# Products by high and low parts: passes on the high part first, and the wait for the low part at its own pass

## The chip, the cores and the metric

The kernel runs on one core of one Trainium2 chip. The metric is the device time of one execution in microseconds (us); three executions of the kernel before gave 998.48, 1000.50 and 1000.87 us, with a median of 1000.5 us. Lower is better.

## What is computed

One decoder layer over x (16 batch rows of 256 tokens, 256 features, float32), with a context of the same shape. Three blocks follow one another, each with a residual:

```python
x = x + causal_linear_attention(layernorm(x)) @ w_proj.T      # block a: 16 heads, chunks of 128
x = x + xattn(layernorm(x), ctx, ctx)                         # block b: cross attention on tanh
                                                              # "probabilities", then an MLP 256-1024-256
x = x + ffn(layernorm(x))                                     # block c: the 128 best-scored tokens of 256 go
                                                              # through attention and a gated MLP 256-682-256
# inside block c
_, idx = top_k(x @ w_router, 128);  x_sel = x[idx]
x_proc = x_sel + x_attn + (silu(h2 @ W1.T) * (h2 @ W2.T)) @ W3.T
out = x.at[idx].set(x_proc)
```

Which tokens are selected depends on small differences of scores, so several products are computed more exactly than one reduced-precision pass would allow.

## The kernel before

**High and low parts.** An operand of such a product is held as two tiles: a high part, the value rounded to the format that TensorE (PE) reads in one go (`..._hi`), and a low part, what the rounding left over (`..._lo`). A product takes three passes: high x high, high x low, low x high (`PASSES`, L1037). Weights are split once at the start. Activations are split each time: ScalarE (ACT) copies the value into the high tile, and then VectorE (DVE) subtracts that from the value to give the low tile. For the input of the attention's output projection the subtraction is done by GpSimd (POOL, `a_ylo_`). So a low part is always ready later than its high part.

**Stages and steps.** All weights stay on chip. One iteration works on one batch row in each block, with blocks a, b and c working on different rows. Each block is cut into named steps (`a_q`, `b_down_0`, `c_scat` and so on). The string `ORDER` lists all steps of an iteration; a "+" behind a name means that the step belongs to a row that started one iteration earlier. Each engine issues its own steps in that order, with waits on semaphores for what other engines deliver. Nothing else sets the order: there is no scheduler. There are three iterations or so of filling up, a hardware loop, and an emptying phase in which block a, then block b have nothing left to do.

**The steps that matter here, on PE.**

- `a_q` (L1072): queries of block a; waits for high part `a_thi`, low part `a_tlo`, then 12 matmuls into bank 1 in two halves. `a_k` and `a_val` follow with the same inputs.
- `a_proj` (L1156): projection of block a; waits for `a_yhi` (ACT) and `a_ylo` (POOL), then 12 matmuls.
- `b_up_j` and `b_down_j` (j = 0 to 3): the MLP of block b, 12 matmuls each. `b_down_j` waits for `b_ghi` and `b_glo`.
- `c_gu_0`: the first piece of the gated MLP, 12 matmuls of 384 columns into banks 6 and 7; waits for `c_h2hi`, `c_h2lo`.
- `c_ff_0`, `c_ff_1`: the last product of the gated MLP, 9 matmuls each; waits for `c_gthi`, `c_gtlo`.
- `c_scat` (L1417): puts the selected rows back at their places by a product with a 0/1 matrix, which has only a high part. There are two output halves of 128 tokens, with a high and a low pass each: 4 matmuls. It waits for `c_yhi` and `c_ylo`.

**Around `c_scat`.** PE runs `c_ff_1`, `a_q`, `c_scat`, `a_k`, in this order. When `c_ff_1` is done, DVE adds the residual (`c_y`, L1002), ACT copies the high part (`c_yhi`), and DVE computes `b_vq` (L835, block b) and then the low part `c_ylo` (L714). DVE goes on with `c_normed` (L729), which needs nothing of PE, then with `c_done` (L1011), which waits for `c_scat`, and with `c_rscore` (L917, the router's scores). In turn PE waits for `c_rscore` before `c_sbc`, and the chain to the next selection goes on from there.

Of the kernel before, what the change touches and what calls it, by code (L numbers as in the profile page):

```python
# [14 lines left out]
B, T, D = 16, 256, 256  # L15
P = 128
TT = T // P
DC = D // P
# [3 lines left out]
FF = 682  # L22
# [82 lines left out]
def decoder(nc, x, ctx_in, ctx_t, consts, vec_bc, vec_cols, w_a, w_proj, w_diff, w_1, w_2, w_cqk, w_cv, w_out, w_gu, w_3, out):  # L105
    ctx = ExitStack()
    with ctx:
# [37 lines left out]
        a_tr = pair("a_tr", [P, DC, T])  # L145
# [24 lines left out]
        b_s0 = pair("b_s0", [P, 512])  # L170
# [31 lines left out]
        c_hs = pair("c_hs", [P, DC, R])  # L202
# [26 lines left out]
        a0, a1, a2, b0, b1, c0, c1, c2 = bank  # L229
# [49 lines left out]
        b_up, b_gelu, b_ghi, b_glo, b_down = sig("b_up", 4), sig("b_gelu", 8), sig("b_ghi", 4), sig("b_glo", 4), sig("b_down", 4)  # L279
# [43 lines left out]
        GATE = ((c1, c2, 0, 3 * P), (c0, c1, 3 * P, FF - 3 * P))  # L323
# [711 lines left out]
        def _(pe):  # L1035
            mm = nc.tensor.matmul
            PASSES = ((0, 0), (0, 1), (1, 0))  # L1037

            def split_product(out_, lhs, rhs, n):

                for a, (p, q) in enumerate(PASSES):
                    for k in range(n):
                        last = mm(out_, lhs(p, k), rhs(q, k), start=a == 0 and k == 0, stop=a == 2 and k == n - 1)  # L1043
                return last
# [21 lines left out]
            def by_features(which, bk):  # L1066
                for m in range(DC):
                    last = split_product(bk[:, m * T:(m + 1) * T],
                                         lambda p, k: wa[p][:, k, which * D + m * P:which * D + (m + 1) * P],
                                         lambda p, k: a_tr[p][:, k, :], DC)  # L1070
                return last

            def a_q_(b):
                weights(b, LOADS_A)
                pe.wait_ge(*a_thi(b))
                pe.wait_ge(*a_tlo(b))
                if not first(b):
                    pe.wait_ge(*a_done(b - 1))
                by_features(0, a1).then_inc(a_qk.sem, 1)

            def a_k_(b):
                by_features(1, a2).then_inc(a_qk.sem, 1)
# [72 lines left out]

            def a_proj_(b):  # L1156
                pe.wait_ge(*a_yhi(b))
                pe.wait_ge(*a_ylo(b))
                for t in range(TT):
                    last = split_product(a1[:, t * D:(t + 1) * D], lambda p, k: a_tr[p][:, k, t * P:(t + 1) * P],  # L1160
                                         lambda p, k: wp[p][:, k, :], DC)
                last.then_inc(a_proj.sem, 1)


            upcoming = iter(range(len(loads)))
# [59 lines left out]
            def mlp_up(j):  # L1225
                def step(b):
                    if j == 0:
                        weights(b, LOADS_A + LOADS_B)
                        pe.wait_ge(*b_hhi(b))
                        pe.wait_ge(*b_hlo(b))  # L1230
                    else:
                        pe.wait_ge(*b_gelu(b, 2 * j))
                    for n in range(2):
                        f = 2 * j + n
                        last = split_product(b0[:, n * T:(n + 1) * T], lambda p, k: w1[p][:, k, f * P:(f + 1) * P],
                                             lambda p, k: b_s0[p][:, k * T:(k + 1) * T], DC)
                    last.then_inc(b_up.sem, 1)
                return step

            def mlp_down(j):  # L1240
                def step(b):
                    part = (b_s2, b_s1)[j % 2]
                    if j == 0:
                        pe.wait_ge(*b_fput(b))
                        if not final(b):
                            pe.wait_ge(*a_scput(b + 1))
                    pe.wait_ge(*b_ghi(b, j + 1))
                    pe.wait_ge(*b_glo(b, j + 1))
                    for t in range(TT):
                        for a, (p, q) in enumerate(PASSES):  # L1250
                            for n in range(2):
                                last = mm(b1[:, t * D:(t + 1) * D], part[p][:, n * T + t * P:n * T + (t + 1) * P],  # L1252
                                          w2[q][:, 2 * j + n, :], start=j == 0 and t == 0 and a == 0 and n == 0,
                                          stop=j == 3 and a == 2 and n == 1, skip_group_check=True)
                    last.then_inc(b_down.sem, 1)
                return step

# [110 lines left out]
            def c_h2tp_(b):  # L1368
# [2 lines left out]
                    last = nc.tensor.transpose(c0[:, c * R:(c + 1) * R], c_h2[:, c * P:(c + 1) * P], ident)  # L1371
                last.then_inc(c_h2tp.sem, 1)

            def gate_product(bk, which, j):
                at, n = GATE[j][2:]
                return split_product(bk[:, 0:n], lambda p, k: c_hs[p][:, k, :],
                                     lambda p, k: wgu[p][:, k, which * FF + at:which * FF + at + n], DC)

            def c_gu_0_(b):
                weights(b, len(loads))  # L1380
                pe.wait_ge(*c_h2hi(b))
                pe.wait_ge(*c_h2lo(b))
                pe.wait_ge(*c_h2put(b))
                gate_product(c1, 0, 0)
                gate_product(c2, 1, 0).then_inc(c_gu.sem, 1)

            def c_gu_1_(b):
                gate_product(c0, 0, 1).then_inc(c_gu.sem, 1)
# [14 lines left out]
            def c_ff_(j):  # L1403
                def step(b):
                    pe.wait_ge(*c_gthi(b, j + 1))
                    pe.wait_ge(*c_gtlo(b, j + 1))
                    if j == 0:
                        pe.wait_ge(*c_gate(b))
                    for a, (p, q) in enumerate(PASSES):
                        for k in range(3 * j, 3 * j + 3):  # L1410
                            last = mm(c1[:, 0:D], act_t[p][:, k, :], w3[q][:, k, :], start=j == 0 and a == 0 and k == 0,
                                      stop=j == 1 and a == 2 and k == 5, skip_group_check=True)
                    if j:
                        last.then_inc(c_ff.sem, 1)
                return step

            def c_scat_(b):  # L1417
                pe.wait_ge(*c_yhi(b))
                pe.wait_ge(*c_ylo(b))
                for t in range(TT):  # L1420
# [78 lines left out]
```

## Time and profile before

| | |
|---|---|
| median of three executions | 1000.5 us |
| the profiled execution | 998.39 us |
| its span, first to last instruction | 996.6 us |
| outside the span | 1.8 us |
| PE busy with matmuls | 862.5 us (87%), 7488 matmuls |
| PE weight loads (overlap the matmuls) | 749.4 us (75%), 7488 loads |
| DVE busy | 718.2 us (72%) |
| ACT busy | 596.5 us (60%) |
| POOL busy | 222.6 us (22%) |
| mean granted clock of PE over the span | 0.969 |
| chain of work that ended last | PE 55%, DVE 27%, issue 9%, ACT 6% |

The chain of work is found by walking back from the last instruction, at each step to what released it. A share of 55% for PE and 27% for DVE says that the end is set by the two in turns: PE in some stretches, DVE in others. In such a chain "issue" is time in which the engine waited for nothing that the profile shows, the way of a semaphore among it. Matmul rows overlap: a row's duration is longer than the distance to the next one's start, and the distance says how fast PE works. The weight loads have rows of their own (PEld).

### The profile page before, as it was taken

The numbers are of one execution on the slowest core, as the hardware profiler recorded it, in microseconds if no ns is written. First come the engines' busy times: TensorE is split into PE (matmuls) and PEld (weight loads), VectorE is DVE, ScalarE is ACT, GpSimd is POOL, SyncE is SP. The second block draws the span as 40 slices with busy tenths as digits, with TensorE's granted clock in tenths as the row PEclk, the third lists the DMA queues.
The fourth block names the chain that finished last, engine by engine and source line by source line (L and its number), as shares of the span: only waits on it lengthen the run. The fifth ranks groups of instructions, "written<-read, shape, count | busy, mean of one in ns | idle before, by whom it ended". The sixth has DMA issues, their size and how long they took to land.

```text
span 996.6 us, 21602 instructions
## 1 busy us (share of the span) xinstructions
PE 862.5 (87%) x7488; PEld 749.4 (75%) x7488; DVE 718.2 (72%) x1670; ACT 596.5 (60%) x1581; POOL 222.6 (22%) x379
## 2 busy tenths in 40 slices
PE   3668898989989998989989998989989998977856
PEld 2547788787969788787969788787969788766745
DVE  4677778787777778787777778787777778664432
ACT  3165666757475766757475766757475766635432
POOL 0121422131312222131312222131312222131100
PEclk9788999999999999999999999999999999998968
DMA  6131000101010100100010100001010100000000
GB/s 227 44 88 32 23 12 12 33 12 32 0 42 0 32 11 11 32 11 32 0 42 0 32 11 11 32 11 32 0 42 0 32 11 21 12 2 11 1 12 11
DMA packets 20320, 25.03 MB, mean 25 GB/s; under 512 B 1472, under 2 KB 17856, under 8 KB 20288
## 3 DMA queue, kind: packets, MB, share of 16 engines
q1 hardware_dynamic: 18848, 20.33, 6.4%
q10 hardware_dynamic: 1440, 4.28, 1.4%
q8 instruction: 19, 0.31, 0.1%
q14 instruction: 13, 0.11, 0.0%
HBM read 20.41 MB, written 4.19 MB: 25 GB/s over the span
## 4 chain that ended last, share of the span: by engine, by line
PE 55%; DVE 27%; issue 9%; ACT 6%; POOL 1%; DMA 1%; DVEq 0%; ACTq 0%; SPq 0%; POOLq 0%
PE bank L1043 15%; PE bank L1252 8%; PE bank L1131 4%; DVE a_s L788 3%; PE bank L1297 3%; PE bank L1217 3%; PE bank L1209 3%; PE bank L1149 2%; PE bank L1285 2%; PE bank L1322 2%; DVE before L929 2%; ACT L602 2%; PE bank L1336 2%; PE bank L1051 2%; PE bank L1111 2%
## 5 line engine op out<-in xcount | busy, mean ns | idle before, releaser
L639 ACT ACTIVATE w_raw_or_stage_c<-bank,c_nmax 128x128 f32<-128x128 f32 x256 | 90.9, 375 | 27.7 <-DVE c_nmax L960 27.7
L960 DVE TENSOR_REDUCE c_nmax<-bank 128x4 f32<-128x512 f32 x64 | 42.2, 682 | 74.9 <-PE bank L1322 74.9
L602 ACT ACTIVATE prob<-bank,b_folded 128x256 f32<-128x256 f32 x128 | 53.7, 471 | 48.6 <-PE bank L1043 46.3
L788 DVE TENSOR_TENSOR a_s<-bank,const 128x512 f32<-128x512 f32 x112 | 71.7, 677 | 13.1 <-PE bank L1131 11.2
L413 POOL TENSOR_TENSOR a_tr_lo<-a_norm,a_tr_hi 128x512 fp32r<-128x512 f32 x16 | 20.7, 1292 | 260.8 <-ACT a_tr_hi L490 260.8
L714 DVE TENSOR_TENSOR b_s_lo<-prob,b_s_hi 128x512 fp32r<-128x512 f32 x64 | 44.1, 690 | 33.6 <-ACT b_s_hi L490 33.6
L1043 PE MATMUL bank<-b_s_hi,w_mlp_hi 128*128 128x256 f32 x256 | 56.8, 304 | 6.4 <-ACT prob L602 5.8
L678 ACT ACTIVATE w_raw_or_stage_c<-bank,c_rms_half 128x384 f32<-128x384 f32 (+1 forms) x32 | 17.5, 547 | 69.6 <-PE bank L1043 46.8
L389 POOL TENSOR_TENSOR x<-x,vectors_by_row 128x512 f32<-128x512 f32 x16 | 21.5, 1344 | 155.1 <-DVE w_raw_or_stage_c L954 155.1
L490 ACT ACTIVATE b_s_hi<-prob 128x512 fp32r<-128x512 f32 x64 | 40.5, 633 | 24.8 <-PE bank L1252 21.0
L639 ACT ACTIVATION_READ_ACCUMULATOR w_raw_or_stage_c<-bank,c_nmax 128x1 f32 x256 | 54.6, 213 | 0.0
L1131 PE MATMUL bank<-qT_by_parity,kT 32*128 32x256 f32 x512 | 38.6, 416 | 17.3 <-DVE a_e L788 9.8
L778 DVE RECIPROCAL a_e<-a_e 128x512 f32<-128x512 f32 x16 | 53.5, 3342 | 0.0
L1252 PE MATMUL bank<-w_mlp_hi,b_s_hi 128*128 128x256 f32 x256 | 52.1, 284 | 0.0
L1252 PE MATMUL bank<-w_mlp_hi,b_s_lo 128*128 128x256 f32 x256 | 50.6, 279 | 0.0
L1043 PE MATMUL bank<-b_s_lo,w_mlp_hi 128*128 128x256 f32 x256 | 50.6, 279 | 0.0
L1252 PE MATMUL bank<-w_mlp_lo,b_s_hi 128*128 128x256 f32 x256 | 50.5, 278 | 0.0
L1043 PE MATMUL bank<-b_s_hi,w_mlp_lo 128*128 128x256 f32 x256 | 50.4, 278 | 0.0
L1043 PEld LDWEIGHTS bank<-b_s_hi,w_mlp_hi 128*128 128x128 f32 x256 | 40.1, 190 | 12.5 <-ACT prob L602 9.7
L1336 PE MATMUL bank<-const,w_raw_or_stage_c 128*128 128x128 f32 x256 | 41.7, 287 | 6.3 <-ACT w_raw_or_stage_c L639 5.4
L490 ACT ACTIVATE w_raw_or_stage_c<-bank 128x512 f32<-128x512 f32 x32 | 19.8, 620 | 43.7 <-PE bank L1336 43.7
L1131 PEld LDWEIGHTS bank<-qT_by_parity,kT 32*128 32x128 f32 x512 | 24.9, 192 | 25.0 <-DVE a_e L788 13.7
(242 smaller groups left out, 2843.1 us busy)
## 6 DMA issues: line engine op xcount, KB each, us to landing
x_in<-in_x SPq DMA_DIRECT2D x16, 256.0 KB, 2.8
qc<-in_ctx SPq DMA_DIRECT2D x16, 256.0 KB, 2.9
b_f<-in_ctx_t SPq DMA_DIRECT2D x16, 256.0 KB, 2.7
out<-w_raw_or_stage_c SPq DMA_DIRECT2D x16, 256.0 KB, 2.2
w_raw_or_stage_c<-in_w ACTq DMA_DIRECT2D x4, 512.0 KB, 5.1
w_raw_or_stage_c<-in_w_gu ACTq DMA_DIRECT2D x4, 341.0 KB, 3.0
w_raw_or_stage_c<-in_w_a SPq DMA_DIRECT2D x2, 384.0 KB, 5.9
w_raw_or_stage_c<-in_w ACTq DMA_DIRECT2D x2, 384.0 KB, 3.3
```

The lines of the kernel that those rows point to most:

```text
L490: act_in(out_, in_, ACT.Copy, scale=scale).then_inc(done.sem, 1)
L602: act_in(prob[:, 2 * (j % 2) + n, :], b0[:, n * T:(n + 1) * T], ACT.Gelu, bias=b1p[:, f:f + 1]).then_inc(b_gelu.sem, 1)
L639: act_in(c_e[g % 2][:, j * R:(j + 1) * R], (c1, c2)[g % 2][:, j * R:(j + 1) * R], ACT.Exp, bias=c_nmax[:, n:n + 1], accum_out=c_den[:, hea ...
L714: tt(out_, full, high.bitcast(F32), ALU.subtract).then_inc(done.sem, 1)
L778: nc.vector.reciprocal(a_e1[:, :], a_e1[:, :]).then_inc(a_dinv.sem, 1)
L788: tt(heads(A_MASKED[t][n][:, :]), heads(A_SCORES[n][:, :]), tri.unsqueeze(1).broadcast_to([P, 4, P]), ALU.mult).then_inc(a_scput.sem, 1)
L960: nc.vector.tensor_reduce(c_nmax[:, 4 * g:4 * g + 4], heads((c1, c2)[g % 2][:, :]), axis=AX.X, op=ALU.max, negate=True).then_inc(c_max.sem, 1)
L1043: last = mm(out_, lhs(p, k), rhs(q, k), start=a == 0 and k == 0, stop=a == 2 and k == n - 1)
L1131: last = mm(A_SCORES[n][:, 2 * c * P:2 * (c + 1) * P], kT[r:r + 32, c, t * P:(t + 1) * P], qM[r:r + 32, c, t, :, :].rearrange("p m q -> p ...
L1209: last = mm(b0[:, m * T:(m + 1) * T], prob[:, k, m * P:(m + 1) * P], prob[:, TT + k, :], start=k == 0, stop=k == DC - 1)
L1252: last = mm(b1[:, t * D:(t + 1) * D], part[p][:, n * T + t * P:n * T + (t + 1) * P], w2[q][:, 2 * j + n, :], start=j == 0 and t == 0 and a ...
L1336: last = nc.tensor.transpose(c0[:, j * R:(j + 1) * R], c_e[g % 2][:, j * R:(j + 1) * R], ident)
```

## The change

A new helper, `some_passes`, runs a given list of passes over all output halves, pass by pass, instead of all three passes of one half and then those of the next. Passes are split into those that read only the high part of the activation and those that read its low part. The wait for the low part moves from the head of the step to the place between the two groups. Matmuls, weight loads, semaphores and the order of the steps are the same in number; only PE's instructions change.

```diff
+            HIGH_LEFT, LOW_LEFT = ((0, 0), (0, 1)), ((1, 0),)
+            HIGH_RIGHT, LOW_RIGHT = ((0, 0), (1, 0)), ((0, 1),)
+
+            def some_passes(passes, outs, lhs, rhs, n, begin=False, end=False):
+
+                for a, (p, q) in enumerate(passes):
+                    for o, out_ in enumerate(outs):
+                        for k in range(n):
+                            last = mm(out_, lhs(o, p, k), rhs(o, q, k), start=begin and a == 0 and o == 0 and k == 0,
+                                      stop=end and a == len(passes) - 1 and k == n - 1, skip_group_check=True)
+                return last
...
             def a_q_(b):
                 weights(b, LOADS_A)
                 pe.wait_ge(*a_thi(b))
+                if not first(b):
+                    pe.wait_ge(*a_done(b - 1))
...
+                some_passes(HIGH_RIGHT, *args, begin=True)
                 pe.wait_ge(*a_tlo(b))
-                if not first(b):
-                    pe.wait_ge(*a_done(b - 1))
-                by_features(0, a1).then_inc(a_qk.sem, 1)
+                some_passes(LOW_RIGHT, *args, end=True).then_inc(a_qk.sem, 1)
...
             def a_proj_(b):
                 pe.wait_ge(*a_yhi(b))
...
+                some_passes(HIGH_LEFT, *args, begin=True)
                 pe.wait_ge(*a_ylo(b))
-                for t in range(TT):
-                    last = split_product(a1[:, t * D:(t + 1) * D], lambda p, k: a_tr[p][:, k, t * P:(t + 1) * P],
-                                         lambda p, k: wp[p][:, k, :], DC)
-                last.then_inc(a_proj.sem, 1)
+                some_passes(LOW_LEFT, *args, end=True).then_inc(a_proj.sem, 1)
...
                     pe.wait_ge(*b_ghi(b, j + 1))
+                    some_passes(HIGH_LEFT, *args, begin=j == 0)
                     pe.wait_ge(*b_glo(b, j + 1))
...
+                    last = some_passes(LOW_LEFT, *args, end=j == 3)
...
             def c_scat_(b):
                 pe.wait_ge(*c_yhi(b))
-                pe.wait_ge(*c_ylo(b))
-                for t in range(TT):
-                    for part in range(2):
+                for part in range(2):
+                    if part == 1:
+                        pe.wait_ge(*c_ylo(b))
+                    for t in range(TT):
                         last = mm(c2[:, t * D:(t + 1) * D], sel_t[:, t * P:(t + 1) * P], flat(c_hs[part][:, :, :]),
-                                  start=part == 0, stop=part == 1)
+                                  start=part == 0 and t == 0, stop=part == 1, skip_group_check=True)
                 last.then_inc(c_scat.sem, 1)
```

`c_gu_0` is rewritten in the same manner (high passes on banks 6 and 7 by turns, wait for `c_h2lo`, low passes on both), and in `c_ff_j` the wait for `c_gtlo` moves ahead of the third pass, with no matmul moved. `b_up_j` changes only the order of its passes; both its waits stay at its head.

First place, on PE: `c_scat` (bank 7) between `a_q` (bank 1) and `a_k` (bank 2). Before:

```order
L1043 MATMUL bank1<-a_tr_hi,w_attn_lo 128x256 x2
L1422 MATMUL bank7<-c_hs_hi,select_by_rank 128x256 [waits c_ylo,c_yhi]
L1422 MATMUL bank7<-c_hs_lo,select_by_rank 128x256
L1422 MATMUL bank7<-c_hs_hi,select_by_rank 128x256
L1422 MATMUL bank7<-c_hs_lo,select_by_rank 128x256
L1043 MATMUL bank2<-a_tr_hi,w_attn_hi 128x256 x2
```

And now on PE, at the same place in the program:

```order
L1047 MATMUL bank1<-a_tr_lo,w_attn_hi 128x256 [waits a_tlo]
L1047 MATMUL bank1<-a_tr_lo,w_attn_hi 128x256 x3
L1448 MATMUL bank7<-c_hs_hi,select_by_rank 128x256 [waits c_yhi]
L1448 MATMUL bank7<-c_hs_hi,select_by_rank 128x256
L1448 MATMUL bank7<-c_hs_lo,select_by_rank 128x256 [waits c_ylo]
L1448 MATMUL bank7<-c_hs_lo,select_by_rank 128x256
L1055 MATMUL bank2<-a_tr_hi,w_attn_hi 128x256 x2
```

Both matmuls on the high part stand ahead of the wait for `c_ylo`, and both on the low part behind it.

Second place, on PE: `a_proj` in the filling phase (bank 1; the tile `a_tr` holds the attention's output here). Before:

```order
L1043 MATMUL bank1<-w_proj_hi,a_tr_hi 128x256 [waits a_ylo,a_yhi]
L1043 MATMUL bank1<-w_proj_hi,a_tr_hi 128x256
L1043 MATMUL bank1<-w_proj_lo,a_tr_hi 128x256 x2
L1043 MATMUL bank1<-w_proj_hi,a_tr_lo 128x256 x2
L1043 MATMUL bank1<-w_proj_hi,a_tr_hi 128x256 x2
```

And now, the whole step on PE:

```order
L1047 MATMUL bank1<-w_proj_hi,a_tr_hi 128x256 [waits a_yhi]
L1047 MATMUL bank1<-w_proj_hi,a_tr_hi 128x256 x3
L1047 MATMUL bank1<-w_proj_lo,a_tr_hi 128x256 x4
L1047 MATMUL bank1<-w_proj_hi,a_tr_lo 128x256 [waits a_ylo]
L1047 MATMUL bank1<-w_proj_hi,a_tr_lo 128x256 x3
```

Eight matmuls stand ahead of the wait for `a_ylo` and four behind it; before, all twelve stood behind it.

## Rows read from the trace of the kernel before

**Rows 1.** One iteration: us, then busy us and count by engine, PE clock.

```profile
499.25:555.32 56.07, 51.85 (x467) 45.52 (x467) 43.59 (x104) 36.56 (x99) 13.57 (x23) 1.00 0.06 19
```

**Rows 2.** PE's waits over the whole span: us in total, times, longest us.

```profile
PE bank L1422 <- DVE c_hs_lo L714: 18.5, 16, 2.4
...
PE bank L1043 <- POOL a_tr_lo L413: 3.9, 2, 3.1
...
PE bank L1043 <- DVE a_tr_lo L714: 1.5, 1, 1.5
...
PE bank L1043 <- DVE c_hs_lo L714: 1.0, 1, 1.0
...
PE bank L1411 <- DVE gated_t_lo L714: 0.8, 1, 0.8
```

**Rows 3.** Chain of work at `c_scat`, iteration of rows 1: start us, us, what.

```profile
554.79 0.39 DVE c_hs_lo L714
555.18 0.14 issue
555.32 0.72 PE bank L1422 x4
```

**Rows 4.** Timeline there: start us, us, engine, line, operation [idle before, releaser].

```profile
554.28 0.42 ACT L490 ACTIVATE c_hs_hi<-c_h 128x256 fp32r<-128x256 f32 x1 [2.85 <-DVE c_h L1002]
...
555.08 0.73 DVE L729 TENSOR_SCALAR w_raw_or_stage_c<-x,c_mv,c_rs 128x256 f32<-128x256 f32 x2
...
555.32 0.35 PE L1422 MATMUL bank<-c_hs_hi,select_by_rank 128*128 128x256 f32 x1 [1.01 <-DVE c_hs_lo L714]
...
555.51 0.28 PE L1422 MATMUL bank<-c_hs_lo,select_by_rank 128*128 128x256 f32 x1
...
555.63 0.28 PE L1422 MATMUL bank<-c_hs_hi,select_by_rank 128*128 128x256 f32 x1
...
555.86 0.41 PE L1043 MATMUL bank<-a_tr_hi,w_attn_hi 128*128 128x256 f32 x2
...
556.06 0.69 DVE L1011 TENSOR_TENSOR w_raw_or_stage_c<-w_raw_or_stage_c,bank 128x512 f32<-128x512 f32 x1 [0.25 <-PE bank L1422]
```

**Rows 5.** Timeline of PE: last pass of `b_up_3`, then `b_down_1` with both waits.

```profile
538.44 0.39 PE L1043 MATMUL bank<-b_s_hi,w_mlp_lo 128*128 128x256 f32 x2
538.67 0.39 PE L1252 MATMUL bank<-w_mlp_hi,b_s_hi 128*128 128x256 f32 x2
538.90 0.39 PE L1252 MATMUL bank<-w_mlp_lo,b_s_hi 128*128 128x256 f32 x2
```

**Rows 6.** Chain of work in the filling phase: first `a_q`, first and second `a_proj`.

```profile
14.36 0.61 ACT a_tr_hi L490
...
15.83 4.86 PE bank L1043 x24
...
41.56 0.64 ACT a_tr_hi L490
...
43.68 2.91 PE bank L1043 x12
...
88.83 0.65 ACT a_tr_hi L490
```

**Rows 7.** Timeline of PE at the second `a_proj`.

```profile
90.97 0.47 PE L1043 MATMUL bank<-w_proj_hi,a_tr_hi 128*128 128x256 f32 x2 [0.77 <-POOL a_tr_lo L413]
```

**Rows 8.** Timeline of the emptying phase: `c_ff_1`, `c_y`, `c_gu_0`, `c_ff_0`.

```profile
943.72 0.59 PE L1411 MATMUL bank<-w_ffn_hi,gated_t_hi 128*128 128x256 f32 x3 [0.79 <-DVE gated_t_lo L714]
...
945.06 0.42 DVE L1002 TENSOR_TENSOR c_h<-bank,c_h 128x256 f32<-128x256 f32 x1 [0.49 <-PE bank L1411]
...
981.04 0.38 ACT L490 ACTIVATE c_hs_hi<-bank 128x256 fp32r<-128x256 f32 x1 [0.16 <-PE bank L1371]
...
981.99 0.59 PE L1043 MATMUL bank<-w_ffn_gu_hi,c_hs_hi 128*128 128x384 f32 x2 [0.98 <-DVE c_hs_lo L714]
...
988.28 0.59 PE L1411 MATMUL bank<-w_ffn_hi,gated_t_hi 128*128 128x256 f32 x3 [0.31 <-issue]
```

More of the change, by code:

```diff
@@ L1075, in a_q_ @@
                 pe.wait_ge(*a_thi(b))
-                pe.wait_ge(*a_tlo(b))
                 if not first(b):
                     pe.wait_ge(*a_done(b - 1))
-                by_features(0, a1).then_inc(a_qk.sem, 1)
+                args = ([a1[:, m * T:(m + 1) * T] for m in range(DC)], lambda m, p, k: wa[p][:, k, m * P:(m + 1) * P],
+                        lambda m, p, k: a_tr[p][:, k, :], DC)
+                some_passes(HIGH_RIGHT, *args, begin=True)
+                pe.wait_ge(*a_tlo(b))
+                some_passes(LOW_RIGHT, *args, end=True).then_inc(a_qk.sem, 1)
             def a_k_(b):
@@ L1157, in a_proj_ @@
                 pe.wait_ge(*a_yhi(b))
+                args = ([a1[:, t * D:(t + 1) * D] for t in range(TT)],
+                        lambda t, p, k: a_tr[p][:, k, t * P:(t + 1) * P], lambda t, p, k: wp[p][:, k, :], DC)
+                some_passes(HIGH_LEFT, *args, begin=True)
                 pe.wait_ge(*a_ylo(b))
-                for t in range(TT):
-                    last = split_product(a1[:, t * D:(t + 1) * D], lambda p, k: a_tr[p][:, k, t * P:(t + 1) * P],
-                                         lambda p, k: wp[p][:, k, :], DC)
-                last.then_inc(a_proj.sem, 1)
+                some_passes(LOW_LEFT, *args, end=True).then_inc(a_proj.sem, 1)
             upcoming = iter(range(len(loads)))
@@ L1232, in step @@
                         pe.wait_ge(*b_gelu(b, 2 * j))
[L1233 to L1237, printed above, removed]
+                    args = ([b0[:, n * T:(n + 1) * T] for n in range(2)],
+                            lambda n, p, k: w1[p][:, k, (2 * j + n) * P:(2 * j + n + 1) * P],
+                            lambda n, p, k: b_s0[p][:, k * T:(k + 1) * T], DC)
+                    some_passes(HIGH_RIGHT + LOW_RIGHT, *args, begin=True, end=True).then_inc(b_up.sem, 1)
                 return step
@@ L1246, in step @@
                             pe.wait_ge(*a_scput(b + 1))
+                    args = ([b1[:, t * D:(t + 1) * D] for t in range(TT)],
+                            lambda t, p, n: part[p][:, n * T + t * P:n * T + (t + 1) * P],
+                            lambda t, p, n: w2[p][:, 2 * j + n, :], 2)
                     pe.wait_ge(*b_ghi(b, j + 1))
+                    some_passes(HIGH_LEFT, *args, begin=j == 0)
                     pe.wait_ge(*b_glo(b, j + 1))
-                    for t in range(TT):
[L1250 to L1254, printed above, removed]
+                    last = some_passes(LOW_LEFT, *args, end=j == 3)
                     last.then_inc(b_down.sem, 1)
@@ L1372, in c_h2tp_ @@
                 last.then_inc(c_h2tp.sem, 1)
+            GATE_ARGS = [(bk[:, 0:GATE[0][3]], lambda p, k: c_hs[p][:, k, :],
+                          lambda p, k, w=w: wgu[p][:, k, w * FF + GATE[0][2]:w * FF + GATE[0][2] + GATE[0][3]])
+                         for w, bk in enumerate((c1, c2))]
             def gate_product(bk, which, j):
@@ L1381, in c_gu_0_ @@
                 pe.wait_ge(*c_h2hi(b))
-                pe.wait_ge(*c_h2lo(b))
-                pe.wait_ge(*c_h2put(b))
-                gate_product(c1, 0, 0)
-                gate_product(c2, 1, 0).then_inc(c_gu.sem, 1)
+                pe.wait_ge(*c_h2put(b))
+                for a, (p, q) in enumerate(HIGH_LEFT):
+                    for bk, lhs, rhs in GATE_ARGS:
+                        for k in range(DC):
+                            mm(bk, lhs(p, k), rhs(q, k), start=a == 0 and k == 0, stop=False, skip_group_check=True)
+                pe.wait_ge(*c_h2lo(b))
+                for p, q in LOW_LEFT:
+                    for bk, lhs, rhs in GATE_ARGS:
+                        for k in range(DC):
+                            last = mm(bk, lhs(p, k), rhs(q, k), start=False, stop=k == DC - 1, skip_group_check=True)
+                last.then_inc(c_gu.sem, 1)
             def c_gu_1_(b):
@@ L1405, in step @@
                     pe.wait_ge(*c_gthi(b, j + 1))
-                    pe.wait_ge(*c_gtlo(b, j + 1))
                     if j == 0:
                         pe.wait_ge(*c_gate(b))
-                    for a, (p, q) in enumerate(PASSES):
+                    for a, (p, q) in enumerate(HIGH_LEFT + LOW_LEFT):
+                        if a == 2:
+                            pe.wait_ge(*c_gtlo(b, j + 1))
                         for k in range(3 * j, 3 * j + 3):
```

1 line of the change is left out of this document (removed).

## The prediction, made before the changed kernel ran

> **What bounds the kernel now.** I read the table of an iteration first. Iterations repeat every 56.07 us and PE has a matmul under way for 51.85 of it, at a granted clock of 1.00 [rows 1]. So PE has some 4 us of gaps per iteration, and whatever closes one counts only if the rest of the loop can follow. Second, I read PE's waits, because the change does nothing but let PE begin before a low part is there. The list is the key to the sum: only one wait for a low part recurs, `c_scat` for `c_hs_lo`, 16 times and 18.5 us in all. The other waits for low parts came once or twice in the whole run: 3.9 us for GpSimd's part at `a_proj`, 1.5 us at `a_q`, 1.0 us at `c_gu_0`, 0.8 us at `c_ff` [rows 2]. In the steady iterations `a_q`, `a_proj`, all `b_down` and `c_gu_0` find their low part ready, so the moved waits there have nothing to give back. Third, the chain of work: it passes through `c_scat`, coming from DVE's low part and going back to DVE [rows 3], so a shorter `c_scat` is worth something there, but only as far as DVE can use it.
>
> **`c_scat`, in each of 16 rows.** The wait of about 1 us does not go away; its end stays where DVE's low part puts it. The high part's copy starts at 554.28 and takes 0.42, so it is there at 554.70 [rows 4]. The way from a finished part to the first matmul is 0.14 [rows 3], so PE could begin the high passes at 554.84. A first matmul after a wait is followed by the next one 0.19 later (555.32 to 555.51), and the further ones at 0.12 (555.51 to 555.63) [rows 4]: both high passes have been issued by 554.84 + 0.19 + 0.12 = 555.15, ahead of 555.32. At 555.32 only two low passes are left. Before, four took from 555.32 to 555.86, where `a_k` begins: 0.54. Two take 0.19 + 0.12 = 0.31. The gain is 0.23 per row, not 1.0.
>
> Can the others use 0.23? DVE stood idle for 0.25 before `c_done`, waiting for `c_scat`; its own `c_normed`, begun at 555.08 and 0.73 long, ends at 555.81, so `c_done` can start at 555.83 instead of 556.06 [rows 4]. It just fits: 0.25 is the most that this place can yield, 0 the least (if something else than `c_scat` holds DVE there). I take 0.23. What follows on DVE (scores, comparison, selection) comes in an unbroken chain, and PE's `a_k` moves by the same 0.23, so nothing overtakes. 16 rows x 0.23 = 3.7 us; bounds 0 and 4.0.
>
> **The filling phase.** These are single places, on the chain of work [rows 6].
> - First `a_q`: the high part ended at 14.36 + 0.61 = 14.97; with 0.14 on top PE can begin at 15.11 instead of 15.83. Eight matmuls don't need the low part, more than fit in the time gained, so no second wait comes. Gain 0.72.
> - First `a_proj`: the high part ended at 42.20, start 42.34 instead of 43.68: gain 1.34. Twelve matmuls took 2.91, so the eight high ones are some 1.9, longer than 1.34, and again GpSimd's low part is there when it is needed.
> - Second `a_proj`: the high part ended at 89.48, while PE was still busy; PE's own idle time before it was 0.77 [rows 7]. Eight matmuls at 0.12 are 0.96, so all of 0.77 is filled. Gain 0.77.
> Together 2.8 us. Lower bound 0, if the weight splitting that shares ACT and DVE in this phase takes over; upper bound 2.8, since that is all the time that there is.
>
> **The emptying phase.** [rows 8] `c_ff_1` waited 0.79 and has six high matmuls, about 0.7; but the DVE addition behind it waited only 0.49, so 0.49 counts. `c_gu_0`: high part at 981.04 + 0.38 = 981.42, start 981.56 instead of 981.99: 0.43. The last `c_ff_0` had 0.31 idle before it, and its high part came before: 0.3. Together 1.2 us, bounds 0 and 1.2. The three `c_scat` here are already among the 16.
>
> **What the moved waits cost where they are met.** Each row of the batch passes ten waits inside a product: one in `a_q`, one in `a_proj`, four in `b_down`, one in `c_gu_0`, two in `c_ff`, one in `c_scat`. The trace of before shows no such wait inside these products, but the nearest thing: between the last pair of `b_up_3` and the first of `b_down_1` stand two waits that are already met, and the distance is 0.23 per pair, as it is one pair later without a wait [rows 5]. So a met wait costs 0. At the other end, if it let the pipe run empty, a matmul would be followed only after its own 0.28 instead of 0.12: 0.16 each [rows 4]. Six of the ten (four `b_down`, `a_proj`, `c_gu_0`) stand in stretches where PE sets the pace: 6 x 16 x 0.16 = 15.4 us. I take 0, because the near row is the same case but for the place of the wait.
>
> The Trainium skill, TensorE: Matmul & The Clock Gate, section Back-to-back issue gap, says that the distance of matmuls is set by weight load and matmul together, pipelined through a reorder window; a wait between them could keep the next load from being pulled ahead. The trace agrees for a wait that is not yet met (0.19 against 0.12 after it) and doesn't for met ones [rows 4, 5].
>
> **The order of the passes.** Output halves now change after every second matmul instead of every sixth, in about 130 matmuls per row; in `c_gu_0` the banks alternate. `c_scat` of before changes its half between 555.51 and 555.63 and the distance is the same 0.12 as inside other products; I take 0. Distances in products of unchanged kind vary from 0.115 to 0.12 [rows 4, 5]; if the new order shifted all by these 5 ns, it would be 130 x 16 x 0.005 = 10 us to either side, which I hold to be unlikely.
>
> **Sum.** 3.7 + 2.8 + 1.2 = 7.7 us. Against the profiled execution, 998.39 (span 996.6 and 1.8 around it), that gives 990.7. The profiled one lies 2.1 under the median shown, 1000.5, from which the same gain gives 992.8. I say 992.
>
> **Rivals.**
> 1. The gain at `c_scat` comes, the single places don't: filling is then paced by the splitting of weights, emptying by other chains. For it: DVE has weight work between all these steps. Against: the chain of work runs through exactly these waits. Gain about 4 us: 996.
> 2. Nothing moves: DVE does not start `c_done` earlier, since 0.25 of slack is thin and any delay of `c_normed` eats it; the iteration stays at 56.07. Some part of the filling gain is left, less than 3 us: 998.5. Against it: DVE waited for `c_scat` in 15 of 16 rows by the same pattern.
> 3. Slower: the waits inside `b_down`, `a_proj` and `c_gu_0`, though met, break the pipe. At 0.08 each (6 x 16 x 0.08 = 7.7) they eat all the gain, and above that the kernel is slower; at 0.16 it is 7.7 slower than before, 1008. Against: rows 5. The skill's rule named above points this way; by it, with 0.07 for each (the 0.19 less the 0.12), the sum would be 6.7 of cost against 7.7 of gain, about no change.
> 4. The change of output half makes matmuls a little slower or faster (up to 10 us either way).
>
> **Chances and range.** Forecast as worked out (989 to 995): 0.58. Rival 1: 0.15. Rival 2: 0.09. Rival 3: 0.10. Rival 4: 0.08, split evenly. A measurement of this kernel can tell about 0.3% from no change, 3 us: faster then means below 997.5. Faster: 0.58 + most of rival 1 (0.11) + 0.04 = 0.73. Same: the rest of rival 1, rival 2 and a third of rival 3, 0.16. Slower: 0.11. The range that should hold 8 in 10 takes in rival 1 and most of rival 2, and below the bounds of the gains: 989 to 998.5.
>
> **What would show it.** Iterations of 55.84 instead of 56.07. At `c_scat` two matmuls on `c_hs_hi` about 0.48 ahead of those on `c_hs_lo`, `a_k` some 0.3 after the latter's start, and DVE's idle time before `c_done` down from 0.25 to nearly 0. The first `a_proj` beginning 0.14 after ACT's copy instead of after GpSimd. Pairs of `b_down` 0.23 to 0.24 apart across the wait; anything above 0.28 at that place would speak for rival 3. An iteration of 56.07 or more, with `c_scat` early all the same, would make the forecast wrong.

## The result and the profile after

The changed kernel took 990.06 us (median of 6 runs) against 999.09 us for the kernel before (6 runs): a ratio of 0.9913, 95% interval 0.9888 to 0.9937. The whole interval lies below 1. The forecast was 992.0 us, from a gain of 7.7 us; the medians differ by 9.0 us, and the profiled span went from 996.6 to 987.4 us, a gain of 9.2.

The iteration first, in the same columns as [rows 1]:

```profile
494.11:549.91 55.80, 52.21 (x467) 45.67 (x467) 43.53 (x105) 36.52 (x99) 13.55 (x24) 1.00 0.06 19
```

PE has as many matmuls as before, in 55.80 us instead of 56.07, at the same granted clock. (Its busy time rose by 0.36 because the rows of the two early matmuls of `c_scat` now cover a part of the wait; in e1 below, which changes `c_scat` alone, it is 52.15.) Its waits over the whole span, which answer to [rows 2]:

```profile
PE bank L1448 <- ACT c_hs_hi L490: 9.7, 16, 1.8
...
PE bank L1047 <- ACT a_tr_hi L490: 2.4, 2, 1.6
...
PE bank L1403 <- ACT c_hs_hi L490: 0.5, 1, 0.5
...
PE bank L1436 <- DVE gated_t_lo L714: 0.2, 1, 0.2
```

`c_scat` (now L1448) waits 9.7 us for the high part instead of 18.5 for the low one. Those 8.8 us of waiting are not the gain: the two low passes still can't run before `c_ylo`. In the kernel before, `c_ylo` of [rows 4] stands in the timeline at

```profile
554.75 0.42 DVE L714 TENSOR_TENSOR c_hs_lo<-c_h,c_hs_hi 128x256 fp32r<-128x256 f32 x1
```

The timeline of the changed kernel at the same `c_scat`, against [rows 4]:

```profile
549.43 0.42 ACT L490 ACTIVATE c_hs_hi<-c_h 128x256 fp32r<-128x256 f32 x1 [2.84 <-DVE c_h L1002]
...
549.90 0.50 PE L1448 MATMUL bank<-c_hs_hi,select_by_rank 128*128 128x256 f32 x2 [0.44 <-ACT c_hs_hi L490]
549.91 0.42 DVE L714 TENSOR_TENSOR c_hs_lo<-c_h,c_hs_hi 128x256 fp32r<-128x256 f32 x1
550.24 0.73 DVE L729 TENSOR_SCALAR w_raw_or_stage_c<-x,c_mv,c_rs 128x256 f32<-128x256 f32 x2
...
550.38 0.50 PE L1448 MATMUL bank<-c_hs_lo,select_by_rank 128*128 128x256 f32 x2
...
550.72 0.40 PE L1055 MATMUL bank<-a_tr_hi,w_attn_hi 128*128 128x256 f32 x2
...
550.92 0.69 DVE L1011 TENSOR_TENSOR w_raw_or_stage_c<-w_raw_or_stage_c,bank 128x512 f32<-128x512 f32 x1
```

Two things became shorter. From the first low matmul to `a_k` it is 0.34 (forecast 0.31), where four matmuls took 0.54: 0.20 less. And the first low matmul starts 0.47 after the start of `c_ylo` (549.91 to 550.38), where `c_scat` before started 0.57 after it (554.75 to 555.32): another 0.10, which the forecast didn't have. Together `a_k` starts 0.81 after `c_ylo` instead of 1.11. `c_done` (L1011) has no idle time before it any more: the 0.25 are used up, and it starts 1.01 after `c_ylo` instead of 1.31. In the nine steady rows from the fourth on, all of these distances lie within 0.01 of the values given.

The chain of work in the filling phase, against [rows 6]:

```profile
14.29 0.61 ACT a_tr_hi L490
14.90 0.14 issue
15.04 2.90 PE bank L1047 x12
...
40.71 0.64 ACT a_tr_hi L490
...
41.40 2.94 PE bank L1047 x12
```

Both steps begin right behind ACT's copy, `a_q` 0.14 after its end and `a_proj` 0.05 (40.71 + 0.64 = 41.35 to 41.40), where before they waited for the low part. PE's timeline in the emptying phase, against [rows 8]; `c_ff_1`, `c_gu_0` and the last `c_ff_0`:

```profile
936.25 0.63 PE L1436 MATMUL bank<-w_ffn_hi,gated_t_lo 128*128 128x256 f32 x3 [0.18 <-DVE gated_t_lo L714]
...
973.61 0.98 PE L1403 MATMUL bank<-w_ffn_gu_hi,c_hs_hi 128*128 128x384 f32 x4 [0.47 <-ACT c_hs_hi L490]
...
979.38 0.60 PE L1436 MATMUL bank<-w_ffn_hi,gated_t_hi 128*128 128x256 f32 x3
```

The waits of 0.79, 0.98 and 0.31 have become 0.18, 0.47 and none.

**A ruler.** DVE computes `c_ylo` once per row, 16 times. Its start times cut every profiled run into filling (up to the first), 12 steady iterations, and emptying (13th to last). All runs told of below, in us, each from one profiled execution; only the ratios rest on several executions:

```
kernel                     first   iteration   13th to last   span    ratio to before, 95% interval
before                    162.41    56.053       156.55       996.6   
changed                   159.58    55.777       153.80       987.4   0.9913 (0.9888 to 0.9937)
e1 c_scat alone           162.34    55.752       156.83       992.9   0.9955 (0.9940 to 0.9970)
e2 all but c_scat         160.07    56.066       155.55       993.4   0.9937 (0.9917 to 0.9956)
e3 order of passes alone  162.59    56.064       157.91       998.2   1.0003 (0.9990 to 1.0017)
e4 16 met waits more      160.88    55.770       153.43       988.2   0.9908 (0.9888 to 0.9929)
e5 c_scat, high part only 159.84    55.737       151.99       984.9   0.9904 (0.9880 to 0.9929)
e6 c_done behind c_sel    160.10    55.668       152.42       985.2   0.9881 (0.9856 to 0.9906)
e7 before, c_done so      162.69    55.942       155.69       994.7   0.9989 (0.9973 to 1.0005)
e8 a_q and a_proj alone   159.23    56.065       157.92       994.9   0.9972 (0.9959 to 0.9985)
e9 c_done behind b_ratio  159.48    55.133       151.62       977.4   0.9808 (0.9792 to 0.9823)
e10 e9, c_sbc before a_k  161.30    56.627       153.36       998.9   1.0061 (1.0040 to 1.0081)
```

For the change: 2.83 in filling, 12 x 0.276 = 3.31 in the steady rows, 2.75 in emptying, and 0.31 behind the last `c_ylo`; together 9.20, the difference of the spans. The forecast in the same parts: 2.8, 12 x 0.23 = 2.8, 1.2 + 3 x 0.23 = 1.9, and 0.23; together 7.7.

### The profile page after: what moved, and what is told of

Its sections match the earlier page's. It is cut to its first block, busy times and chain, and to the rows that moved or that the text cites. A ratio compares the mean times of both kernels' runs of the same rounds, so it can differ in the third digit from the quotient of the medians.

```text
span 987.4 us, 21478 instructions
## 1 busy us (share of the span) xinstructions
PE 868.0 (88%) x7488; PEld 752.6 (76%) x7488; DVE 717.1 (73%) x1670; ACT 595.9 (60%) x1581; POOL 222.1 (22%) x379
## 4 chain that ended last, share of the span: by engine, by line
PE 56%; DVE 27%; issue 9%; ACT 6%; DMA 1%; POOL 0%; ACTq 0%; DVEq 0%; SPq 0%; POOLq 0%
PE bank L1047 21%; PE bank L1146 4%; DVE a_s L788 4%; PE bank L1310 3%; PE bank L1232 3%; PE bank L1224 3%; PE bank L1403 2%; PE bank L1298 2%; PE bank L1335 2%; DVE before L929 2%; PE bank L1164 2%; PE bank L1063 2%; ACT L602 2%; PE bank L1349 2%; PE bank L1126 2%
## 5 line engine op out<-in xcount | busy, mean ns | idle before, releaser
L1047 PE MATMUL bank<-b_s_hi,w_mlp_hi 128*128 128x256 f32 x256 | 46.4, 303 | 7.0 <-ACT prob L602 5.7
L1047 PEld LDWEIGHTS bank<-b_s_hi,w_mlp_hi 128*128 128x128 f32 x256 | 35.6, 189 | 12.8 <-ACT prob L602 9.7
L389 POOL TENSOR_TENSOR q_bias<-b_f,vectors_by_row 128x512 f32<-128x512 f32 x16 | 20.3, 1267 | 94.8 <-DVE b_f L854 94.8
L1047 PE MATMUL bank<-w_mlp_hi,b_s_hi 128*128 128x256 f32 x256 | 41.6, 284 | 0.0
L1349 PEld LDWEIGHTS bank<-const,w_raw_or_stage_c 128*128 128x128 f32 x256 | 29.0, 144 | 16.5 <-ACT w_raw_or_stage_c L639 8.5
L714 DVE TENSOR_TENSOR c_hs_lo<-bank,c_hs_hi 128x256 fp32r<-128x256 f32 x16 | 6.8, 424 | 46.5 <-ACT c_hs_hi L490 46.5
L1047 PE MATMUL bank<-w_mlp_hi,b_s_lo 128*128 128x256 f32 x256 | 40.3, 279 | 0.0
```

What stands on the lines that cost most here:

```text
L389: add_bc = lambda out_, in_, vec: nc.gpsimd.tensor_tensor(out_, in_, vec.unsqueeze(1).broadcast_to([P, TT, D]), ALU.add)
L714: tt(out_, full, high.bitcast(F32), ALU.subtract).then_inc(done.sem, 1)
L1047: last = mm(out_, lhs(o, p, k), rhs(o, q, k), start=begin and a == 0 and o == 0 and k == 0, stop=end and a == len(passes) - 1 and k == n - ...
L1349: last = nc.tensor.transpose(c0[:, j * R:(j + 1) * R], c_e[g % 2][:, j * R:(j + 1) * R], ident)
```

## Experiments

**e1: `c_scat` alone.** The kernel before, with the last hunk of the change and nothing else.

```diff
                 pe.wait_ge(*c_yhi(b))
-                pe.wait_ge(*c_ylo(b))
-                for t in range(TT):
-                    for part in range(2):
+                for part in range(2):
+                    if part == 1:
+                        pe.wait_ge(*c_ylo(b))
+                    for t in range(TT):
```

> The kernel before with the change at c_scat alone (both passes on c_hs_hi ahead of the wait for c_ylo). Theory (the gain is made of c_scat in every row and of single places in filling and emptying): iterations of 55.78 to 55.80 us instead of 56.05, so 12 x 0.27 = 3.3 us over the steady rows and some 0.7 more in emptying; a time 4 us under before, ratio 0.996. Rival A (the gain of the iteration comes from the new order of the passes in all products): iterations stay at 56.05, ratio 1.000. Rival B (all of the gain comes from c_scat): ratio 0.991.

Measured: iteration 55.752, ratio 0.9955. The whole gain of the iteration is `c_scat`'s, and it is about half of the gain in all. The 0.7 us that I expected in emptying did not show: 156.83 against 156.55 before. The mean granted clock from 885 to 935 us was 0.88 there and 0.93 before, so that these two numbers can't be set against each other to better than about 1 us.

**e2: all but `c_scat`.** The changed kernel with `c_scat` put back.

```diff
-                for part in range(2):
-                    if part == 1:
-                        pe.wait_ge(*c_ylo(b))
-                    for t in range(TT):
+                pe.wait_ge(*c_ylo(b))
+                for t in range(TT):
+                    for part in range(2):
```

> The changed kernel with c_scat as before (both waits at its head, four matmuls behind them). Theory: iterations back at 56.05 us; the filling and emptying phases keep their gains (about 2.8 us before the first c_scat, about 1.9 after the steady rows), ratio 0.995 to 0.996. With e1 the two gains add up to that of the whole change, 9 us. Rival A (order of the passes): iterations stay at 55.80, ratio 0.991. Rival B: ratio 1.000.

Measured: iteration 56.066, so the moved waits in `a_q`, `a_proj`, `b_down`, `c_gu_0` and `c_ff` give nothing in steady rows; yet the ratio is 0.9937, from filling and emptying. (In the one profile 2.34 and 1.00 us came there, where I expected 2.8 and 1.9; that profile is of the slowest of the six executions, 995.2 us against a median of 992.73.) The gains of e1 and e2, 0.45% and 0.63%, add up to 1.08%, and the whole change gave 0.87% with an interval of 0.25 to either side: additive within the measurement.

**e3: the order of the passes alone.** The changed kernel with every wait for a low part at the head of its step; of six such edits, one:

```diff
+                pe.wait_ge(*a_ylo(b))
                 some_passes(HIGH_LEFT, *args, begin=True)
-                pe.wait_ge(*a_ylo(b))
```

> The changed kernel with every wait for a low part back at the head of its step; the passes keep their new order. Theory (only the place of the wait matters): iterations of 56.05 us, filling and emptying as before, ratio 0.999 to 1.001. Rival A (changing the output half every two matmuls makes PE faster): iterations well under 56.0, ratio under 0.997. Rival C (the change of output half costs PE something that the early start hid): iterations over 56.1, ratio over 1.002.

The iteration of that kernel:

```profile
498.97:555.02 56.05, 51.85 (x466) 45.52 (x466) 43.59 (x104) 36.53 (x99) 13.54 (x24) 1.00 0.06 19
```

Not only the length but PE's busy time is that of [rows 1]: 51.85. Changing the output half every two matmuls costs nothing and gives nothing. Ratio 1.0003. The order inside `c_scat` is tested with it: with both waits at its head and the passes in their new order, `a_k` starts 1.11 after `c_ylo`, as before.

**e4: more met waits.** The changed kernel, with a wait on `b_ghi`, long reached, ahead of four of the six pairs of matmuls of each `b_down_j`, 16 per row (`some_passes` gets it as `again`; the first pair of the high and of the low passes has none):

```diff
+                        if again and (a or o):
+                            pe.wait_ge(*again)
                         for k in range(n):
```

> The changed kernel with 16 waits more per row inside the b_down products, one ahead of every second pair of matmuls, each on a semaphore that has already been reached. Theory (a met wait inside a product costs nothing): iterations of 55.80 us, ratio to before 0.991 as for the changed kernel. Rival (a met wait breaks the pipe of weight loads and matmuls, 0.07 to 0.16 us each): 16 x 0.07 = 1.1 us per iteration and more, 56.9 us or above, ratio 1.009 to 1.03.

Iteration 55.770, ratio 0.9908. PE's timeline there. The first three rows are `b_down_0`, four matmuls each: a further wait stands in the middle of each, and one ahead of the second. The fourth row is `a_proj`, without further waits:

```profile
530.86 0.72 PE L1049 MATMUL bank<-w_mlp_hi,b_s_hi 128*128 128x256 f32 x4
531.42 0.63 PE L1049 MATMUL bank<-w_mlp_lo,b_s_hi 128*128 128x256 f32 x4
531.89 0.63 PE L1049 MATMUL bank<-w_mlp_hi,b_s_lo 128*128 128x256 f32 x4
532.36 0.63 PE L1049 MATMUL bank<-w_proj_hi,a_tr_hi 128*128 128x256 f32 x4
```

And the same stretch of the changed kernel, without them:

```profile
529.54 0.72 PE L1047 MATMUL bank<-w_mlp_hi,b_s_hi 128*128 128x256 f32 x4
530.10 0.63 PE L1047 MATMUL bank<-w_mlp_lo,b_s_hi 128*128 128x256 f32 x4
530.57 0.64 PE L1047 MATMUL bank<-w_mlp_hi,b_s_lo 128*128 128x256 f32 x4
531.04 0.63 PE L1047 MATMUL bank<-w_proj_hi,a_tr_hi 128*128 128x256 f32 x4
```

The distances are 0.56, 0.47, 0.47 in both, and the iterations differ by less than 0.01 us. With the steady iteration of e2, in which the nine other moved waits of a row cost 0.01 us at most (56.066 against 56.053), rival 3 of the prediction is out.

**e5: `c_scat` with the high part alone.** The changed kernel; the two low passes and the wait for `c_ylo` are left out of the computation, so the selected rows get only their high part.

```diff
-                for part in range(2):
-                    if part == 1:
-                        pe.wait_ge(*c_ylo(b))
-                    for t in range(TT):
+                for t in range(TT):
```

> The changed kernel without the two low passes of c_scat (left out: what the low part adds to the selected rows); c_scat waits for the high part alone and PE never waits for c_ylo. Theory (after the change DVE itself, with c_ylo, c_normed and c_done one behind the other, sets the pace at this place): iterations stay within 0.05 of 55.78 us although c_scat now ends some 0.7 us earlier, ratio to before about 0.990. Rival (c_scat still holds DVE or PE there): iterations shorter by another 0.2 us or more, 55.55 or less, ratio 0.987 or less.

Iteration 55.737, only 0.04 less. In its timeline PE goes on to `a_k` at once:

```profile
550.00 0.51 PE L1445 MATMUL bank<-c_hs_hi,select_by_rank 128*128 128x256 f32 x2 [0.44 <-ACT c_hs_hi L490]
550.34 0.39 PE L1055 MATMUL bank<-a_tr_hi,w_attn_hi 128*128 128x256 f32 x2
```

But DVE's `c_done` still starts behind `c_normed`:

```profile
550.34 0.73 DVE L729 TENSOR_SCALAR w_raw_or_stage_c<-x,c_mv,c_rs 128x256 f32<-128x256 f32 x2
550.99 0.68 DVE L1011 TENSOR_TENSOR w_raw_or_stage_c<-w_raw_or_stage_c,bank 128x512 f32<-128x512 f32 x1
```

`a_k` starts 0.34 behind the first matmul of `c_scat` instead of 0.82 (549.90 to 550.72), so 0.48 earlier (I had expected 0.7), and next to nothing comes of it: `c_done` starts 0.98 after `c_ylo` instead of 1.01. The change has taken all but 0.04 of what a shorter `c_scat` can give: from here on DVE's own queue sets the pace.

**e6: `c_done` later in DVE's queue.** The changed kernel, two lines of `ORDER`:

```diff
-... a_kout a_k c_sbc c_done+ c_rscore a_rstd ...
+... a_kout a_k c_sbc c_rscore a_rstd ...
-... a_phi_k c_sel b_ratio b_rtp ...
+... a_phi_k c_sel c_done+ b_ratio b_rtp ...
```

> The changed kernel with one word of ORDER moved: DVE does c_done behind c_sel instead of ahead of c_rscore, so that the scores do not wait behind an addition of 0.6 us that only the store and c_qk need. Theory (DVE's queue from b_o to c_sel sets the pace): the selection comes up to 0.6 us earlier per iteration, as far as PE's gaps in that stretch (some 0.8 us) allow: iterations of 55.2 to 55.5 us, ratio to before 0.982 to 0.987. Rival (the time is given back: c_done delays c_qk, or the store delays c_ob through out_done): iterations of 55.7 us or more, ratio 0.991 or more.

Iteration 55.668, ratio 0.9881: better than the change alone, but by 0.11 and not by the 0.3 to 0.6 that I expected. That is nearer to the rival (the time is given back, 55.7 or more) than to the theory. PE's timeline shows where it was given back:

```profile
500.15 1.16 PE L1298 MATMUL bank<-select_scaled,w_raw_or_stage_c 128*128 128x128 f32 x8 [0.28 <-DVE select_scaled L937]
501.35 0.66 PE L1063 MATMUL bank<-const,b_f 128*128 128x128 f32 x4
502.31 1.38 PE L1310 MATMUL bank<-c_hT,w_ffn_qk 128*128 128x128 f32 x10 [0.31 <-ACT c_hT L490]
```

`c_ht` (L1298) did start about 0.6 earlier: 6.03 after `c_ylo`, in the changed kernel 6.65. Then `c_qk` (L1310) waited for a copy by ACT, which has this copy behind another one of block b, which waits for DVE's `b_ratio`, which now stood behind `c_done`.

**e7: the same move in the kernel before.** The edit of e6 on the kernel before.

> The kernel before (c_scat waits for both parts at its head) with c_done moved behind c_sel in the same way. Theory (the early c_scat helps because c_done, ahead of the scores in DVE's queue, waits for it): with c_done out of the way DVE no longer waits for c_scat, so this kernel's iteration is as long as that of the changed kernel with c_done late, within 0.1 us; most of what c_scat early gave is had without it. Rival (c_scat early helps through PE's own queue, a_k and c_sbc behind it): this kernel's iteration is longer than the other's by 0.2 to 0.3 us.

Iteration 55.942, against 55.668 with the early `c_scat`: 0.274 apart, so the rival was right and my theory wrong. With `c_done` out of the way DVE doesn't wait for `c_scat`, and the early `c_scat` is still worth as much as before. The waits of an iteration show the way that it goes. DVE's in e7:

```profile
DVE before L929 <- PE bank L1264: 0.2, 1, 0.2
```

DVE's comparison waits there for `c_sbc` (L1264), which stands in PE's queue behind `c_scat` and `a_k`. In the changed kernel it is the other way round: `c_sbc` (L1277 there) waits for DVE's scores, as in the kernel before:

```profile
PE bank L1277 <- DVE c_sc L917: 0.2, 1, 0.2
```

So two ways lead from `c_scat` to the selection, over DVE's queue and over PE's, and the longer one counts. Starts in us after the start of `c_ylo`, the median of nine steady rows:

```
                          a_k   c_rscore  c_sbc  comparison  c_sel  c_qk
before                    1.11    1.91    2.87     3.61      6.30   8.59
changed                   0.81    1.61    2.56     3.31      6.00   8.29
e7 before, c_done late    1.11    0.98    2.52     2.94      5.64   8.46
e6 changed, c_done late   0.81    0.98    2.23     2.68      5.37   8.19
```

From the scores (`c_rscore`) to the comparison it is 1.70 in three of these kernels: there DVE's own queue sets the comparison's time, and the 0.30 of the change come over DVE. Only in e7 it is 1.96: moving `c_done` makes DVE's way 0.93 shorter, and PE's is then the longer one by 0.26. There the early `c_scat` takes these 0.26 away. Of the 0.6 that the moved `c_done` gives at `c_sel`, some 0.1 is left at `c_qk`, with the early `c_scat` and without it.

**e8: `a_q` and `a_proj` alone.** The kernel before with these two hunks of the change and the helper.

> The kernel before with a_q and a_proj changed alone. Theory (these two have something to gain only in the filling phase): iterations of 56.05 us, the first low part of c_scat 2.8 us earlier than before (162.4 to about 159.6), emptying as before, ratio 0.997. Rival (weight splitting takes the filling phase over): first low part of c_scat at 161.5 or later, ratio 0.999 to 1.000.

First `c_ylo` at 159.23, 3.2 earlier; iteration 56.065; ratio 0.9972. The gain of the filling phase is that of these two steps. Emptying took 157.92 where before has 156.55, though nothing was to change there; more on that below.

**e9: `c_done` behind `b_ratio`.** One place later than in e6:

```diff
-... a_phi_k c_sel c_done+ b_ratio b_rtp ...
+... a_phi_k c_sel b_ratio c_done+ b_rtp ...
```

> The changed kernel with c_done one place later than in the run before it: behind b_ratio instead of behind c_sel. In that run (iteration 55.67) c_sel came 0.6 us earlier, and then c_done stood ahead of b_ratio in DVE's queue, ACT's copies of block b and of c_hT came behind b_ratio, and PE's c_qk waited 0.3 for c_hT. Theory (only that place gave the time back): c_qk starts 0.5 to 0.6 us earlier, iterations of 55.1 to 55.3 us, ratio to before 0.981 to 0.984. Rival (PE's own queue from c_scat to c_ht is the bound by now): iterations of 55.6 us or more, ratio 0.988 or more.

Iteration 55.133, ratio 0.9808, median 979.87 us. DVE's queue there:

```profile
495.65 0.60 DVE L937 TENSOR_SCALAR select_scaled<-const,c_rank_col,c_rms 128x128 f32<-128x128 f32 x2
496.19 0.69 DVE L846 TENSOR_TENSOR b_f<-prob 128x512 f32<-128x512 f32 x1
496.80 0.68 DVE L1011 TENSOR_TENSOR w_raw_or_stage_c<-w_raw_or_stage_c,bank 128x512 f32<-128x512 f32 x1
```

And `c_qk` on PE, now without a wait:

```profile
497.31 0.60 PE L1063 MATMUL bank<-const,b_f 128*128 128x128 f32 x4
497.94 1.27 PE L1310 MATMUL bank<-c_hT,w_ffn_qk 128*128 128x128 f32 x9
```

The copies by ACT no longer stand behind `c_done`, and `c_qk` starts 7.66 after `c_ylo` instead of 8.19 in e6: 0.53, of the 0.54 by which the iteration is shorter. The 0.6 us of this addition have left the path. This version beats both kernels. How much of it the new place of `c_done` would give without the early `c_scat`, no run shows.

**e10: `c_sbc` ahead of `a_k`.** e9 with

```diff
-... a_kout a_k c_sbc c_rscore ...
+... a_kout c_sbc a_k c_rscore ...
```

> The same with PE's c_sbc (two transposes of the scores) ahead of a_k instead of behind it. If PE's a_k is what holds the comparison of scores back, this is shorter than the run with c_done behind b_ratio alone by 0.2 us per iteration or more. If DVE sets the pace there (c_rscore, b_diff, c_before one behind the other), c_sbc comes no earlier to any use, PE waits for c_rscore with a_k standing behind it, and the iteration is longer by 0.2 to 1.0 us.

Iteration 56.627, ratio 1.0061. PE's waits in an iteration of it:

```profile
PE bank L1277 <- DVE c_sc L917: 1.0, 1, 1.0
```

`c_sbc` waits 1.0 us for the scores while `a_k`, which could run, stands behind it. The comparison gains nothing by it (2.68 after `c_ylo` in e9 and in e10), but `c_sel` comes 0.49 later. `a_k` is the cover of that wait; taking it away costs more than the whole change gave: 1.49 per iteration against e9, and more than the 1.0 at most that I expected. Where the part beyond the wait arises was not followed up.

## Why the prediction was right

- **What bounds the kernel.** Right: the loop follows PE and DVE in turns, and only the recurring wait at `c_scat` counts per row. e1 and e2 show it from both sides.
- **`c_scat`, 0.23 per row and at most 0.25.** The mechanism was right, the size too small: 0.276 per iteration, 3.3 us over the 12 steady ones where 2.8 was forecast. The two passes gave 0.20 of the 0.23 (0.34 left instead of 0.31). The mis-sized term is the way from a finished part to PE. I took 0.14 [rows 3] for both parts and let the end of the wait stay where it was. In the changed kernel it is 0.05 for the high part (549.85 to 549.90) and 0.05 for the low part too (549.91 + 0.42 = 550.33 to 550.38), and the latter gives some 0.1 more per row. Why the way is shorter there, no run shows. That the two starts are 0.48 apart, just as forecast, is luck: both came some 0.1 earlier. The upper bound, DVE's idle time, was too small as well. I let `c_normed` end at 555.81, by its row of 0.73, but in e5 `c_done` starts 0.65 behind it (550.34 to 550.99), since DVE's rows overlap. By that `c_done` could start 0.33 earlier, not 0.25, which fits the 0.28 measured and the 0.04 left over in e5.
- **DVE as the user of the gain.** Right for this change: `c_done`, the scores, the comparison and the selection all come 0.30 earlier, and PE's `c_sbc` waits for the scores before and after. PE's own way, `a_k` and `c_sbc`, I took to follow along. It does, but it is close behind, and once `c_done` is out of DVE's way it is the one that counts (e7).
- **Filling, 2.8.** 2.83 measured, and 3.2 with `a_q` and `a_proj` alone. The agreement is better than the method, and in part luck: from `b_o` of the first row (L878) to its comparison (109.38 us in the kernel before) the changed kernel was 3.5 us ahead, and at 121.16 us 2.8. In these 12 us the same 79 matmuls kept PE busy for 11.57 us at a mean granted clock of 0.89 before the change, and for 12.49 us at 0.79 after it.
- **Emptying, 1.2 besides the three `c_scat`.** Too small, on what the two profiles show: 2.75 to the last `c_ylo` where 1.9 was forecast. Of the three distances between `c_ylo` in this phase the last is 0.94 shorter (forecast 0.96), the middle one 0.87 (forecast 0.72), but the first 0.94 where only 0.23 was forecast. In the first lies a pause of PE that is no wait for a low part, 0.7 shorter in the changed kernel (below). That it is the reason isn't shown. Single profiles don't resolve this phase to better than about 1 us: e3 and e8, which have no low part to win there, took 157.9 where before has 156.55, with a mean granted clock of 0.86 from 885 to 935 us against 0.93 (before and changed). The executions as a whole say that something is gained there: e2 gave 0.35% more than e8, with some 0.23% to either side.
- **Met waits cost 0.** Right, by e4 with sixteen of them, and by the steady iteration of e2. The rule of the Trainium skill (TensorE: Matmul & The Clock Gate, section Back-to-back issue gap) that I had set against it, loads and matmuls pipelined through a window, is not at odds with that: a met wait doesn't close the window by any time that these runs can see.
- **Order of the passes costs 0.** Right, by e3: its iteration is 56.064 against 56.053, and PE's busy time is 51.85 in both.
- **Rivals.** Rival 1 (single places give nothing) is refuted by e2 and e8, rival 2 by the iteration, rival 3 by e4 and e2, rival 4 by e3.
- **The number.** 992 against 990.06. I took it from between 990.7 (the profiled execution of before) and 992.8 (the median of three executions, 1000.5; six put it at 999.09), so the start was some 0.6 too high, and the gain was 9.0 and not 7.7. The 1.3 us that the gain was short lie in `c_scat` and in emptying.

## What to carry over

When the end of a wait is fixed by another engine, what an early start saves is the work that is moved ahead of it, and no more than the idle time of whoever waits behind. Multiply the matmuls moved by their distance, not the wait by its count: here 18.5 us of waits became 9.7, and the gain was 0.28 per row. Look also at how soon the engine starts behind the wait: it was 0.14 in some places here and 0.05 in others, and that was a third of the gain per row. Once such an edit leaves the next engine without idle time, look along that engine's queue for work that nobody on the path needs: moving one addition of 0.6 us by a few places gave 0.64 per iteration on top, more than the change itself. But follow every queue that stands behind its new place (e6), and leave an independent step in front of a wait that it covers (e10).

## What was not expected of the hardware

Some 2 us into the first code behind the hardware loop PE stopped for a time that ended on no semaphore. In the kernel before, in the middle of a step (`a_att_1`) whose waits stand ahead of the first matmul of this group:

```profile
866.03 0.30 PE L1149 MATMUL bank<-a_s,v_even 128*32 128x128 f32 x1 [1.42 <-issue]
```

In the changed kernel, some ten matmuls further on:

```profile
859.21 0.30 PE L1358 MATMUL bank<-w_raw_or_stage_c,c_v_even 128*32 128x128 f32 x2 [0.74 <-issue]
```

e1, e3, e7 and e8 had 1.1 there, e4 0.74, and e2 1.42. What the traces do show is a transfer that goes with it. The queue that the page of the profile calls "instruction" (q8) carries 12 packets of 16 KB up to 235 us in the kernel before, none from there to 862 us, while the loop runs, and 7 afterwards. The first of these falls at about 863.4 us, and the pause ends at 866.03. In the changed kernel it falls at about 856.8, and the pause ends at 859.21. In all twelve profiled kernels this packet comes 2.3 to 2.8 us ahead of the pause's end. So it may be that PE waits for its own instructions at this place, and the longer, the sooner it has used up those at hand; no run tests that. PE's instructions differ in number and place among these kernels, so the 0.7 us between before and changed can't be put down to the moved waits, nor be said to have nothing to do with the edit.

The granted clock of the filling phase differed between the two profiles, in the same stretches, in the columns of [rows 1]. Before:

```profile
0.00:62.00 62.00, 32.46 (x253) 27.54 (x254) 37.66 (x67) 22.99 (x46) 10.14 (x16) 0.88 0.36 123
62.00:106.00 44.00, 34.21 (x272) 28.83 (x271) 32.30 (x67) 24.02 (x44) 11.59 (x19) 0.86 0.17 48
```

After:

```profile
0.00:62.00 62.00, 36.80 (x257) 30.96 (x258) 39.11 (x69) 24.15 (x47) 10.14 (x16) 0.82 0.38 129
62.00:106.00 44.00, 30.90 (x272) 26.86 (x271) 34.19 (x75) 23.88 (x43) 13.83 (x23) 0.93 0.14 41
```

0.88 and 0.86 against 0.82 and 0.93: the mean lies between the two levels of 1.2 and 2.4 GHz, so PE spent other parts of the phase at the lower one. The steady iterations are at 1.00 in both, and there the profiles agree to some hundredths of a microsecond.
